# A quantised feed-forward with its rounding offset kept through fp32 transposes, three norms on GpSimd, and the work around it reordered

## The reference, cut to what matters

```python
x = x + tanh(g_xattn[0]) * xattn0(layernorm(x), ctx)       # "l0": 16 heads, 77 context rows
x = x + tanh(g_ffn[0]) * ffn0(layernorm(x), w_gate, w_up, w_down)                    # "f0"
x = x + tanh(g_xattn[1]) * xattn1(layernorm(x), ctx, ...)  # "ln1", "a1" (causal self-attention), ..., "a2"
x = x + tanh(g_ffn[1]) * ffn1(layernorm(x), Wr, W1, b1, W2, b2)                      # "f1"

def act_quant(x):      # per token
    scale = 127.0 / clip(max(abs(x), axis=-1), 1e-5)
    return clip(round(x * scale), -128, 127) / scale
def bitlinear(x, w): return einsum('bsi,oi->bso', act_quant(x), ternary(w))
def ffn0(x, w_gate, w_up, w_down):
    return bitlinear(silu(bitlinear(x, w_gate)) * bitlinear(x, w_up), w_down)
```

## Time and profile before

| | |
|---|---|
| three runs | 376.3, 376.02, 376.49 us; median 376.3 |
| profiled execution | span 375.9 us from the first to the last instruction (its own device time is not listed apart; the runs lie 0.1 to 0.6 us above this span) |
| instructions | 6947 |
| busy shares | PE 87%, PEld 62%, DVE 76%, ACT 72%, POOL 33% |
| mean granted TensorE clock | 0.975 of full speed |

### The profile page before, as it was taken

How to read it: one execution, slowest core, us unless ns; L and a number is a source line. 1 busy time by engine, 2 the same in 40 slices (tenths; PEclk the granted TensorE clock), 3 DMA queues, 4 the chain that set the end, 5 groups by cost and what they waited for, 6 DMA issues and landing times. The chain is left out here.

```text
span 375.9 us, 6947 instructions
## 1 busy us (share of the span) xinstructions
PE 326.4 (87%) x2168; PEld 232.8 (62%) x2168; DVE 286.7 (76%) x737; ACT 270.9 (72%) x956; POOL 122.7 (33%) x227
## 2 busy tenths in 40 slices
PE   4989999626689789899989999989898999988993
PEld 4867988513334555555555576666674898765673
DVE  0768768697878997979879999885578977856516
ACT  2378899738355899989899999944248998954441
POOL 1316574325621332323333333331022534511100
PEclk9999999976899899999999999999999999999999
DMA  6900000000009959601990697100000000000001
GB/s 209 364 7 1 2 1 2 0 1 2 2 12 201 214 119 214 139 2 37 211 201 3 132 211 197 81 2 0 2 0 3 1 2 2 2 0 2 0 2 56
DMA packets 6908, 24.75 MB, mean 66 GB/s; under 512 B 1451, under 2 KB 1528, under 8 KB 6136
## 3 DMA queue, kind: packets, MB, share of 16 engines
q1 hardware_dynamic: 6872, 24.31, 26.9%
HBM read 7.00 MB, written 0.52 MB: 20 GB/s over the span
## 5 line engine op out<-in xcount | busy, mean ns | idle before, releaser
L1245 ACT ACTIVATE pring<-ps,nm 128x512 f32<-128x512 f32 x128 | 88.8, 722 | 5.7 <-DVE nm L1656 5.7
L1656 DVE TENSOR_REDUCE nm<-ps 128x1 f32<-128x512 f32 x128 | 80.9, 677 | 10.5 <-PE ps L704 10.4
L1122 ACT ACTIVATE arena<-ps,nmx 128x77 f32<-128x77 f32 x256 | 79.1, 345 | 10.5 <-DVE nmx L1421 10.1
L1010 POOL TENSOR_SCALAR_AFFINE_SELECT pring<-pring 128x128 f32<-128x128 f32 x128 | 37.5, 295 | 80.1 <-ACT pring L1245 80.1
L704 PE MATMUL ps<-stack 128*128 128x512 f32 x128 | 53.7, 485 | 4.5 <-DMA stack<-hid 2.3
L1122 ACT ACTIVATION_READ_ACCUMULATOR arena<-ps,nmx 128x1 f32 x256 | 57.6, 225 | 0.0
L975 POOL TENSOR_TENSOR arena<-arena,rden 128x616 f32<-128x616 f32 x32 | 39.2, 1226 | 50.9 <-DVE rden L1430 50.9
L444 PE MATMUL ps<-ident,pring 128*128 128x128 f32 x320 | 48.5, 281 | 5.6 <-ACT early L1217 1.9
L444 PEld LDWEIGHTS ps<-ident,pring 128*128 128x128 f32 x320 | 37.2, 143 | 21.4 <-POOL pring L1010 11.1
L571 PEld LDWEIGHTS ps<-arena 128*128 128x128 f32 x320 | 38.9, 191 | 12.4 <-DVE arena L1437 10.9
L571 PE MATMUL ps<-arena 128*128 128x128 f32 x320 | 42.4, 279 | 4.6 <-DVE arena L1437 4.6
(11 more groups left out here) (150 smaller groups left out, 525.4 us busy)
## 6 DMA issues: line engine op xcount, KB each, us to landing
stack<-sides SPq DMA_DIRECT2D x32, 256.0 KB, 5.1
...
```

The costliest lines, as they stand in the source:

```text
L1010: pool.affine_select(out=blk, in_=blk, compare_op=ALU.is_gt, fill=0.0, base=0, pattern=[[1, P]], channel_multiplier=-1).then_inc(masked, 1)
L1122: ins = act.activation(Pc[:, i % PC_SLOTS, h * HS:h * HS + M], bank(where[key])[:, h % 4 * HS:h % 4 * HS + M], ACT.Exp, bias=nmx[:, i % 4, ...
L1245: release(act.activation(pring[:, n % 2, i, :], bank(f"S{i}"), ACT.Exp, bias=nm1[:, n % 8, i:i + 1], accum_out=den1[:, n % 8, i:i + 1]), ( ...
L1656: dve.tensor_reduce(nm1[:, n % 8, i:i + 1], bank(f"S{i}"), AX.X, ALU.max, negate=True).then_inc(nm1_ready, 1)
```

## The change

- **The offset stays on.** `hqb`, `xqb`, `x_to_bf16` and POOL's eight L999 are gone. TensorE transposes the fp32 values that still hold `MAGIC` (`xq_transposes`, `hidden_transposes`, through the fp32 identity), and ACT's copy from PSUM takes `MAGIC` off with `bias=-MAGIC` and writes bf16. A hidden tile is transposed and copied in the tile step after its rounding (before: two later on PE).
- **POOL takes over.** `round_x(b)` (before on ACT) and three norms (before on DVE): `ln_norm("f0", 1)`, `ln_norm("a1", 0)`, `ln_norm("a1", 1)`, each four 128x128 instructions `(src + nmean) * rstd`, with a 128x4 instruction `negate_mean` ahead of them.
- **DVE.** In `cross("l0")`, `l0_out(0)` comes at unit 11 (12 before), the statistics of f0 batch 0 all at unit 12 (halves at 13 and 14), its norm at 13 (15) and `scale_x(0)` at 14 (15). In f0, the first, second, sixth, seventh and eighth tiles take their clip and reciprocal at once; `f0_out(0)` comes behind tile 5 (6 before), the ln1 norm behind tile 6, the a1 statistics ahead of tile 7. `f0_out(1)` and `ln_stats("ln1", 1)` move from before the four low halves to behind `copy_values(1)`.
- **PE and ACT.** `gate_up(4)` and `silu(4)` move to step 2, right behind x of batch 1. The last hidden tile's transposes and down product stand among the a1 transposes and projections. Filler: 4 + 4 + 3 matmuls in place of 6 + 2 + 2 + 4 + 4. The projections' banks are S0, S2, S1, S3 (S0, S2, A, B before); `copy_values(0)` comes ahead of the table load for Exp.

```diff
             def xq_transposes(b):
-                pe.wait_ge(xq_ready, b + 1)
-                res = ("A", "T0")[b]
-                claim(pe, res, ("xq", b), read_by=(xqT_ready, b + 1))
-                for t in range(NT):
-                    m = pe.transpose(bank16(res)[:, t * P:(t + 1) * P], xqb[:, b, t * P:(t + 1) * P], identb[:, :])
-                filled(m, ("xq", b))
+                pe.wait_ge(xround_ready, b + 1)
+                claim(pe, "AB"[b], ("xq", b), read_by=(xqT_ready, b + 1))
+                transposes(("xq", b), "AB"[b], lambda t: xn[:, b, t, :], NT)
+            def hidden_transposes(n):
+                pe.wait_ge(hround_ready, n + 1)
+                res = f"T{n % 2}"
+                claim(pe, res, ("hq", n), read_by=(hqT_ready, n + 1))
+                transposes(("hq", n), res, lambda k: h_in[:, n % 4, k * P:(k + 1) * P], NF)
+            def f0_down(n):
+                b, t = n // NT, n % NT
+                pe.wait_ge(hqT_ready, n + 1)
+                res = out_bank("f0", b)
+                if t == 0:
+                    pe.wait_ge(wq_ready, 3)
+                    claim(pe, res, ("out", "f0", b), filled_by=(f0_done, n + NT))
+                for k in range(NF):
+                    m = pe.matmul(bank(res)[:, t * P:(t + 1) * P], hqT[:, n % 2, k * P:(k + 1) * P],
+                                  wf0b[:, 2, k * P:(k + 1) * P], start=(k == 0), stop=(k == NF - 1))
+                filled(m, ("out", "f0", b))
...
-            gate_up(1)
-            for n in range(NB * NT + 4):
-                if 1 <= n < NB * NT - 1:
+            for n in range(1, NB * NT):
+                if n + 1 < NB * NT and n != 3:
                     gate_up(n + 1)
-                if n >= 4:
-                    j = n - 4
-                    b, t = j // NT, j % NT
-                    pe.wait_ge(hqT_ready, j + 1)
-                    res = out_bank("f0", b)
-                    if t == 0:
-                        pe.wait_ge(wq_ready, 3)
-                        claim(pe, res, ("out", "f0", b), filled_by=(f0_done, j + NT))
-                    for k in range(NF):
-                        m = pe.matmul(bank(res)[:, t * P:(t + 1) * P], hqT[:, j % 2, k * P:(k + 1) * P],
-                                      wf0b[:, 2, k * P:(k + 1) * P], start=(k == 0), stop=(k == NF - 1))
-                    filled(m, ("out", "f0", b))
-                if 3 <= n < NB * NT + 3:
-                    j = n - 3
-                    pe.wait_ge(hq_ready, j + 1)
-                    claim(pe, f"T{j % 2}", ("hq", j), read_by=(hqT_ready, j + 1))
-                    for k in range(NF):
-                        m = pe.transpose(bank16(f"T{j % 2}")[:, k * P:(k + 1) * P],
-                                         hqb[:, j % 2, k * P:(k + 1) * P], identb[:, :])
-                    filled(m, ("hq", j))
+                if n >= 2:
+                    f0_down(n - 2)
+                hidden_transposes(n - 1)
                 if n == 2:
                     xq_transposes(1)
-                if n == NB * NT:
-                    keep_busy(6)
-                if n > NB * NT:
-                    keep_busy(2 if n < NB * NT + 3 else 4)
+                    gate_up(4)
+                if n == NB * NT - 1:
+                    keep_busy(4, "S1")
+            f0_down(NB * NT - 2)
+            keep_busy(4, "S1")
...
             ln_transposes("a1", 0)
-            keep_busy(4)
-            for m in range(4):
-                project(m, ("S0", "S2", "A", "B")[m])
-            for t, res in enumerate(("T0", "T1", "S1", "S3")):
+            hidden_transposes(NB * NT - 1)
+            keep_busy(3, "S1")
+            project(0, "S0")
+            project(1, "S2")
+            f0_down(NB * NT - 1)
+            project(2, "S1")
+            project(3, "S3")
+            for t, res in enumerate(("T0", "T1", "A", "T0")):
                 project_values(t, res)
             keep_busy(6, "S0")
...
+            def round_x(b):
+                pool.wait_ge(xscale_ready, b + 1)
+                for t in range(NT):
+                    ins = pool.tensor_scalar(xn[:, b, t, :], xn[:, b, t, :], ainv[:, b, t:t + 1], MAGIC,
+                                             ALU.mult, ALU.add)
+                ins.then_inc(xround_ready, 1)
+            negated = [0]
+            def negate_mean(site, b):
+                pool.wait_ge(var_ready, nth(site, b))
+                pool.tensor_scalar(nmean[:, b, :], mv[:, b, :, 0], -1.0, 0.0, ALU.mult, ALU.add)\
+                    .then_inc(nmean_ready, 1)
+                negated[0] += 1
+            def ln_norm(site, b, src):
+                pool.wait_ge(nmean_ready, negated[0])
+                pool.wait_ge(rstd_ready, nth(site, b))
+                for t in range(NT):
+                    ins = pool.tensor_scalar(xn[:, b, t, :], src[:, b, t, :], nmean[:, b, t:t + 1],
+                                             rstd[:, b, t:t + 1], ALU.add, ALU.mult)
+                ins.then_inc(xn_ready, 1)
...
+                    if site == "l0" and j == 11:
+                        power("f0", batches=[0])
                     if site == "l0" and j == 13:
-                        power("f0", batches=[0])
+                        round_x(0)
...
+            negate_mean("f0", 1)
             power("f0", batches=[1])
-            for j in range(NB * NT):
-                pool.wait_ge(hround_ready, j + 1)
-                if j >= 2:
-                    await_bank(pool, ("hq", j - 2))
-                pool.tensor_scalar(hqb[:, j % 2, :], h_in[:, j % 4, :], MAGIC, None, ALU.subtract).then_inc(hq_ready, 1)
-                if j == 5:
-                    power("ln1", batches=[0])
+            ln_norm("f0", 1, r)
+            round_x(1)
+            power("ln1", batches=[0])
+            negate_mean("a1", 0)
             power("a1", batches=[0])
+            ln_norm("a1", 0, x1)
...
+                if n == 1:
+                    ln_norm("a1", 1, x1)
...
-                release(act.activation(xqT[:, b, :], bank16(where["xq", b])[:, 0:TOK], ACT.Copy), ("xq", b))
+                release(act.activation(xqT[:, b, :], bank(where["xq", b]), ACT.Copy, bias=-MAGIC), ("xq", b))
...
+            for n in range(1, NB * NT):
+                round_hidden(n - 1)
+                if n + 1 < NB * NT and n != 3:
                     silu(n + 1)
-                if n == 2:
-                    round_x(1)
-                    x_to_bf16(1)
-                if n >= 3:
-                    j = n - 3
-                    if j >= 2:
-                        act.wait_ge(f0_done, j - 1)
-                    res = await_bank(act, ("hq", j))
-                    release(act.activation(hqT[:, j % 2, :], bank16(res)[:, 0:HID], ACT.Copy), ("hq", j))
-                if 1 <= n <= NB * NT:
-                    j = n - 1
-                    act.wait_ge(hscale_ready, j + 1)
-                    act.activation(h_in[:, j % 4, :], h_in[:, j % 4, :], ACT.Copy, bias=MAGIC,
-                                   scale=hinv[:, j // NT, j % NT:j % NT + 1]).then_inc(hround_ready, 1)
+                hidden_evac(n - 1)
                 if n == 2:
                     xq_evac(1)
+                    silu(4)
+            round_hidden(NB * NT - 1)
...
+            hidden_evac(NB * NT - 1)
             for m in range(4):
                 high_half(m)
+            copy_values(0)
             preload(ACT.Exp)
-            copy_values(0)
             copy_values(2)
...
+            def hidden_behind(n):
+                hidden(n)
+                hidden_clip(n - 1)
+                hidden_max(n)
+                hidden_scale(n - 1)
+            hidden(0)
+            hidden_max(0)
+            hidden_scale_alone(0)
+            l0_out(1)
+            ln_stats("f0", 1, r)
+            hidden(1)
+            hidden_max(1)
+            hidden_scale_alone(1)
+            scale_x(1)
+            hidden(2)
+            hidden_max(2)
+            hidden_behind(3)
+            hidden_behind(4)
+            hidden_behind(5)
+            hidden_scale_alone(5)
+            f0_out(0)
+            ln_stats("ln1", 0, r)
+            hidden(6)
+            hidden_max(6)
+            hidden_scale_alone(6)
             ln_norm("ln1", 0, r, ("ln1_g", "ln1_b"), x1)
+            ln_stats("a1", 0, x1)
+            hidden(7)
+            hidden_max(7)
+            hidden_scale_alone(7)
...
-            ln_stats("a1", 0, x1)
-            ln_norm("a1", 0, x1)
-            f0_out(1)
-            ln_stats("ln1", 1, r)
             for m in range(4):
                 low_half(m)
             copy_values(1)
+            f0_out(1)
+            ln_stats("ln1", 1, r)
             copy_values(3)
...
                     copy_values(value_tile(n))
                 if n == 0:
                     ln_stats("a1", 1, x1)
-                if n == 2:
-                    ln_norm("a1", 1, x1)
                 if n == HG + 1:
                     a1_evac_context(1)
                 if n >= HG and n < NHB and n % HG == 3:
```

104 lines of the change are left out of this document (49 added, 55 removed).

## The result

The changed kernel takes 378.51 us (median of 11 runs, 376.64 to 380.16), the kernel before 376.37 (11 runs beside it, 376.02 to 379.63): a ratio of 1.0052, 95% interval 1.003 to 1.0073. It is slower by 2.1 us; the forecast was 374.4, faster by 1.9. The profiled execution took 378.52 us with a span of 376.8; in each of the 11 runs 1.7 to 1.8 us lie outside the span.

A forecast was written before the change was run, and what follows sets the result against it. It took the start of self-attention's head 0, behind one long chain, and the pace to head 3 as the bound. Gains 0.6 + 1.3 = 1.9 us: span 375.9 to 374.0, plus 0.4 is 374.4; range 371.8 to 377.2.

The forecast's parts named there:

- The median of the runs lies 0.4 above the span: Last step of the sum: 0.4 us added to the predicted span of 374.0, giving 374.4.
- Projections and stack: From the a1 layer's transposes to the first stack DMA: last projection at 107.6, DMA at 108.1, 2.7 us earlier.
- the clock falls ahead of the projections: Rival, 12 in 100: projections at half clock, head 0's row maxima 1.7 to 2.4 later, 376.1 to 376.8 us.
- a1 transposes: TensorE's transposes ahead of the projections: start at 103.2 instead of 106.01, 2.8 us earlier.
- The first hidden product: Start of the chain on DVE: about 74.2 instead of 75.44, 1.2 us earlier.
- Gate·up of tile 4: TensorE's product behind x of batch 1: 85.1 instead of 86.83, 1.7 us earlier, with GpSimd's tiles at 0.30 each.
- the prediction's other estimate: GpSimd's 128x128 tile by the skill's cycle accounting: 0.37 instead of 0.30 us, result 375.2.
- ln1's passes: Two DVE passes of batch 0, 1.47 and 1.49 us before: 2.3 for both with L999 gone.
- the give-back at head 0: `f0_out(1)` and statistics, 3.0 us, now behind the low halves: head 0's row maxima at 117.0, only 0.6 us earlier.
- heads 0 to 3: First self-attention heads: DVE loses a 1.10 us norm, TensorE's 2.3 us DMA wait goes; 1.3 us gained.
- at my bound: Sign of a wrong forecast: a new DVE wait for GpSimd's norm longer than 1 us beyond the power.
- The collision: Batch 1's ln1 on DVE beside GpSimd's power: 0.35 us counted in the range; by the skill 0.6, result 375.0.

The follow-up runs named there:

- e0: The kernel before, unchanged, run to read the span of every run: 376.55 us, ratio 0.9993.
- e1: The changed kernel with more filler ahead of the transposes of hidden tile 6 and of a1: 377.17 us, ratio 1.002.
- e14: The changed kernel unchanged, run and profiled a second time: 378.07 us, ratio 1.0034 to the kernel before.
- e2: The changed kernel with the last hidden tile's work earlier and `f0_out(1)` with ln1's batch 1 statistics ahead of the low halves: 376.74 us, ratio 0.9996.
- e15: The changed kernel with the a1 norm of batch 1 on DVE behind head 2: 379.45 us, ratio 1.0086.
- e11: The changed kernel with only the added filler from 75 to 88 us: 377.89 us, ratio 1.0015.
- e3: The changed kernel with the norms of f0 batch 1 and a1 batch 0 back on DVE: 379.5 us, ratio 1.0054.
- e5: The changed kernel with the edits of e1 and e2 together, and filler from 75 to 88 us too: 374.41 us, ratio 0.9928.
- e8: e5 with half of the rounding of x batch 1 on ACT and half of the a1 batch 0 norm on DVE: 373.91 us, ratio 0.9919.
- e6: The changed kernel in its own order with the filler of e5: 376.1 us, ratio 0.997.
- e10: e7 with `f0_out(1)` and ln1's batch 1 statistics behind the low halves and first copy of values: 378.35 us, ratio 1.0072.
- e7: The kernel before with filler added in the same stretch: 376.48 us, ratio 0.9985.
- e4: The changed kernel with the edits of e1 and e2 together: 377.58 us, ratio 1.0014.
- e12: e5 unchanged, run again on another chip: 374.73 us, ratio 0.9942.

## Why the prediction was wrong

378.5 - 374.4 = 4.1 us. Three steps failed, by 1.3, 1.6 and 1.4 us. That is 4.3; the heads gave 0.2 more than forecast, and the steps between were right within 0.1.

**"The median of the runs lies 0.4 above the span": 1.3 us.** I set the profiled execution beside runs that were shorter than it. Outside the span lie 1.7 us (e0), so from this profile's span the sum should have ended at 374.0 + 1.7 = 375.7. The forecast gain of 1.9, counted from a typical execution, would again have given 374.5 to 374.6, but part of that gain was the cure of something that a typical execution does not have: the 2.30 us wait at 124.59 is 1.42 us in e0's profile, and the half clock behind it, which I meant to remove, is absent there: 1.00 from 121 to 128 us. That the same working gave 106.35 for the a1 transposes of before, where the trace has 106.01, could not show this error, since it was held against the same long execution.

**"Projections and stack", 4.9 us from the transposes to the first DMA: 1.6 us.** Measured: 6.51. The rival "the clock falls ahead of the projections" came in, which I gave 12 in 100 because filler stands in the gap. e1 and e14 show the step without the fall, 4.86 and 4.87 us, so the fall costs 1.6 to 1.7 us. What failed is "filler stands in that gap, which speaks against it": behind the filler TensorE still stood idle for 1.97 us ahead of the a1 transposes, 0.74 before. I had read the stretch's instructions and not the idle time that the new order leaves between them. But the length of that gap alone does not decide the clock. It fell behind gaps of 1.97 (changed), 2.98 (e2), 3.57 (e15) and 3.58 us (e11), and did not behind 2.10 (e3), 2.34 (e14) and 2.51 (e1). What decides it stays open. More filler goes with a lower median: 377.17 in e1, 378.51 and 378.07 in the two sets of runs of the changed kernel; e1's interval of ratios ends where the first set's begins, and overlaps the second's. The rival's price was near (1.7 to 2.4; measured 1.6), yet it reached 376.1 to 376.8 only, since the other two errors come on top. Of its 12 chances in 100 the prediction counted 5 as slower than before, which those times, at most 0.5 above 376.3, do not give by its own mark of 0.75 us.

**"a1 transposes", 103.2: 1.4 us.** Measured: 104.61. The first hidden product was even earlier than forecast (73.78 for 74.2). Gate·up of tile 4 followed 11.9 us later for 10.9, the a1 transposes 7.1 us after ln1 for 6.4. GpSimd's four tiles took 1.43 (the rounding) and 1.73 us (each norm) where I had 1.2, and 0.18 of its own wait in front of each norm, which I had put at nothing. Over the three groups that is 1.65 us, all of the two excesses (1.0 and 0.7). The half clock had no part in it beyond what the forecast counted: with full clock (e5) the transposes of x come 10.12 us behind the first hidden product, as here, and the a1 transposes 7.12 us behind ln1. So the tile was mis-sized: 0.37 for the rounding and 0.45 for the norm instead of 0.30. The rounding tile is at the prediction's other estimate, 0.37; the norm's is just under the 0.46 at which it expected no gain. It doesn't follow that GpSimd was the wrong place: e3, with the norms on DVE, has no earlier x and 0.28 us at the a1 transposes, and e8 brings x 0.66 us forward by sharing the rounding.

**Right:** ln1's passes at 1.12 and 1.14 us without L999 beside them (forecast 2.3 for both); between ln1 and `f0_out(0)` 4.5 as forecast; the give-back at head 0, 2.1 us between stack transfer and row maxima, measured 2.11 (2.35 - 0.24), and shown from both sides by the profiles of e6 against e5 (2.4) and e10 against e7 (1.8); heads 0 to 3, 1.53 for 1.3, of which 0.6 was the clock of the profile before. Its reason was half right. The wait for a stack DMA is gone, and DVE has lost the norm: against e0, which has no half clock there, heads 0 to 3 gain 0.97 us. But TensorE waits 2.44 us for ACT's exponentials in front of 121.53 instead, and the half clock comes too (0.57 from 122 to 126 us), at no cost here: 11.41 us from head 0 to head 3, 11.40 in e5 at full clock. In e4 and e12, where the fall begins at about 124 us, the heads take 13.63 and 13.05. DVE waited for GpSimd's norm 1.01 us, at my bound.

The collision didn't come: ln1 of batch 1 starts at 117.64 beside GpSimd's power (117.21 to 118.22) and takes 1.13 us, as without it. By the Trainium skill (SBUF — State Buffer, "Who interferes with whom") the two would have shut each other out for the whole instruction; the measurement decides against that for this 128x4 instruction, as far as the profile's times of GpSimd, which are rough, place it: neither the start nor the length of ln1 shows a wait.

What is left: with the filler of e6 and e7 the change is worth 0.4 us in its own order, within the noise, and 2.1 in e5's. A gain of the size forecast came only with the filler and the early `f0_out(1)` together; the kernel as changed has neither. Why the kernel before loses only 0.13 us to its half clock, where the changed one loses 1.15, was not taken apart; its bf16 transposes, which come two tile steps behind, may explain it. That ACT's one copy with the offset is worth what the forecast says was not tried by itself.
